# Attention one: a later shift transposition, another order of the first scores, and other waits for the stack loads

## The chip, the cores and the metric

One core of a Trainium2 chip runs the whole program. The time is the device time of one execution in microseconds (us). TensorE (PE) multiplies and transposes, VectorE (DVE), ScalarE (ACT) and GpSimd (POOL) do the rest, SyncE (SP) issues the transfers.

## What is computed

A small language model tower: a token table lookup, attention one, a mixture of experts, attention two, and a feed-forward part with block-quantised values. Only attention one is touched:

```python
h = _L0_tok_ref(x, L0_tok_W)                       # 8 x 1024 tokens, 256 wide
h = h + _L0_attn_ref(_layernorm(h, axis=-1), Wqkv, bqkv, Wr, br)

def _L0_attn_ref(x, Wqkv, bqkv, Wr, br):           # 16 heads of 16
    xh = x.reshape(b, c, h, he).transpose(0, 2, 1, 3)
    qkv = jnp.einsum('bhce,ef->bhcf', xh, Wqkv) + bqkv
    q, k, v = jnp.split(qkv, 3, axis=-1)
    att = jnp.einsum('bhqe,bhke->bhqk', q, k) / jnp.sqrt(jnp.float32(he))
    mask = jnp.tril(jnp.ones((c, c), dtype=att.dtype), k=-1)
    att = jax.nn.softmax(att * mask, axis=-1)      # masked scores are 0, not minus infinity
    out = jnp.einsum('bhqk,bhke->bhqe', att, v)
    return out.transpose(0, 2, 1, 3).reshape(b, c, d) @ Wr + br
```

The masked scores count as zeros in the softmax, so the kernel needs each row's maximum over the scores in front of the diagonal and zero, and a term for the sum of all later values.

## The kernel before

Attention one handles 8 batches in two halves of eight heads each, 16 halves in all, and each half as two groups of four heads (HPG). `window` (L93) writes one pass over a group as a list of events, `plan` (L166) puts the passes together (an even one, gi = 0, then an odd one, gi = 1; the loop runs 14 halves), and each engine's program walks the same list in order. A pass has 32 positions. Position 4·kt + hh holds the score step S(kt, hh): key block kt of 128 keys against all later queries, in two units (128·kt to 512, and 512 to 1024) for kt < 4 and in one for the others, 48 units in all (`score_units`, L56). TensorE writes a unit into one of two `scoresT` banks (L638), ScalarE takes its exponential into `probs` (L495), GpSimd masks the diagonal block (L415), and the value product PV(kt) (L652) follows one key block later. PV(7) runs behind the first step of the next pass.

Between the steps, at positions given by `AT`, the list places the rest:

- MX: the scores of queries against keys for the row maxima, two heads (a pair) at a time, 9 banks for each head, into a ring of four PSUM banks (L688, masks L674), reduced by VectorE (L587). `bank_free` makes the matmul of each use of the ring wait until the use four before it has been read. XT, QK, V, SUF, PT, OT, WR and CT use the same ring in the same order.
- MAX_FINAL: VectorE reduces to m (L577), GpSimd splits m in two bf16 parts c1 and c2 and adds them to cf (L451, L453, L455). CT: TensorE transposes c1, c2 of a pair (L721) after waiting for cf (`cm_ok`), VectorE copies it to `ct` (L591) and SyncE puts it as shift rows into the query stack Qs of the next pass (L359). EQ: ScalarE takes exp(-cf) (L526).
- In an even pass: the layer norm of the next half (VectorE's statistics, GpSimd's rstd, VectorE's xn L564), its transposition XT (L702), the Q/K projection QK (L706) with ScalarE's copies to `f32part` and `parts` (L512, L513), V (L709), the suffix sums SUF (L716, L718). PT (L726) transposes the value products of the pass before, WR (L734, odd passes) is the output projection.
- LOAD: SyncE writes the next pass's stacks Qs and Ks from `parts` in 24 transfers (L337). It waits for `parts` and until TensorE has done the first 8 score units of the running pass. LOAD_MAX: four transfers of 128 KB fill Qm and Km of one pair (L354, L355), after VectorE's m of that pair.

The stacks Qs and Ks have two buffers, one for each pass. Before the first step that uses a pair of heads (S(0,0), S(0,2)) TensorE waits for that pair's stack loads and shift rows. Before it overwrites `parts` for the next half, ScalarE waits at its first QK copy until all loads that read the old `parts` have landed:

```python
if w == 0 and c == 0:
    act.wait_ge(w_in, 16 * WEIGHTS)
    for s in stack_in:
        wait(act, s, 16 * 12 * 2 * (hb + 1))
```

That copy comes behind position 8 of an even pass, and the loads of the odd pass's stacks are issued in the same even pass. SUF lies behind position 9; its second bank is the one that this copy must free.

Of the kernel before, what the change touches and what calls it, by code (L numbers as in the profile page):

```python
# [17 lines left out]
P = 128  # L18
B, S, D = 8, 1024, 256
# [3 lines left out]
TPB = S // P  # L23
HEADS, HE = 16, 16
HALVES = 2 * B
HPG = 4
# [6 lines left out]
PAIRS_MX = HPG // 2  # L33
# [17 lines left out]
MAX_BANKS = len(MAX_PLAN)  # L51
FUTURE = -2.0 ** 126
SCORE_BANKS, RING_BANKS = 2, 4


def score_units(kt, hh):  # L56

    if kt < TPB // 2:
        u = 2 * (HPG * kt + hh)
        return [(u, P * kt, 512), (u + 1, 512, S)]  # L60
    return [(TPB * HPG + HPG * (kt - TPB // 2) + hh, P * kt, S)]


STAGE = 2 * HPG * S
UNITS = TPB * HPG + TPB // 2 * HPG
# [4 lines left out]
def wait_apart(eng, *waits):  # L70


    values = [value if isinstance(value, int) else eng.to_reg(value) for _, value in waits]
    if not all(isinstance(value, int) for value in values):
        eng.wait_ge(waits[0][0], 1)
    for (sem, _), value in zip(waits, values):
        eng.wait_ge(sem, value)
# [4 lines left out]


AT = {
    0: {"LN_STATS": 1, "LN_NORM": 3, "XT": 6, "PV_COPY": 0, "TMP": 0, "PT": 5, "OT": 21, "WR": 22, "RSUM": 5, "SUF": 9, "QK": 8, "QK_STEP": 2, "MID_LAG": 2, "V": 12, "VG": 0, "LOAD": 11, "MX": 6, "MX_END": 29, "MX_CURVE": 1.2},
    1: {"PV_COPY": 0, "TMP": 0, "PT": 2, "WR": 1, "V": 8, "VG": 6, "LOAD": 6, "MX": 3, "MX_END": 28, "MX_CURVE": 1.2},
    "V_IN": 0, "WR_IN": 1,
}
ALONE = {"LN_STATS": 0, "LN_NORM": 1, "XT": 2, "QK": 8, "QK_STEP": 1, "MID_LAG": 1, "V": 12, "PV_COPY": 1, "TMP": 2, "PT": 5, "OT": 11,
# [3 lines left out]
def window(gi, ot, wr, tail, prologue, v, scores, following, load_max=False):  # L93


    others = {}
    pos_of = AT[gi] if scores else ALONE

    def at(pos, *events):
        others.setdefault(min(pos, 31), []).extend(events)  # L100

    if prologue:
        at(pos_of["LN_STATS"], ("LN_STATS",))
        at(pos_of["LN_NORM"], ("LN_NORM",))
        at(pos_of["XT"], ("R", "XT", "act", 0), ("R", "XT", "act", 1))
    if tail:
        at(pos_of["PV_COPY"], ("PV", -1, 7), ("PV_COPY", -1))
        at(pos_of["TMP"], ("TMP", -1))
        at(pos_of["PT"], ("R", "PT", "dve", -1, 0), ("R", "PT", "dve", -1, 1), ("OM", -1))
    if ot:  # L110
        at(pos_of["OT"], ("R", "OT", "act", 0), ("R", "OT", "act", 1))
    if wr:
        for j in range(4):
            at(pos_of["WR"] + (j // 2 if scores else 0), ("R", "WR", "dve", j))
    if gi == 0 and scores:
        at(pos_of["RSUM"], ("RSUM",))
        at(pos_of["SUF"], ("R", "SUF", "dve", 0), ("R", "SUF", "dve", 1))
    if prologue:
        for n in range(4):
            at(pos_of["QK"] + n * pos_of["QK_STEP"], ("R", "QK", "act", n // 2, n % 2))  # L120
            at(pos_of["QK"] + n * pos_of["QK_STEP"] + pos_of["MID_LAG"], ("MID", n // 2, n % 2))
    if v:
        at(pos_of["V"], ("R", "V", "dve", 0), ("R", "V", "dve", 1))
    if following:
        at(pos_of["VG"], ("VG",))
        at(pos_of["LOAD"], ("LOAD",))
        if not scores:
            at(pos_of["LOAD"], *(("LOAD_FIRST", p) for p in range(PAIRS_MX)))
        uses = []
        for p in range(PAIRS_MX):  # L130
            for k in range(MAX_BANKS):
                uses.append([("R", "MX", "dve", 2 * p, k), ("R", "MX", "dve", 2 * p + 1, k)])
                if p and k == 3:
                    uses[-1] += [("R", "CT", "dve", p - 1)]
                if p and k == 4 and load_max:
                    uses[-1] += [("LOAD_MAX", p - 1)]
            uses[-1] += [("MAX_FINAL", p)]
        uses.append([("R", "CT", "dve", PAIRS_MX - 1), ("EQ",)] + ([("LOAD_MAX", PAIRS_MX - 1)] if load_max else []))
        lo, hi = pos_of["MX"], pos_of["MX_END"]
        for n, u in enumerate(uses):  # L140
            at(int(lo + (hi - lo) * (n / len(uses)) ** pos_of["MX_CURVE"]), *u)
    events = []
    for pos in range(32 if scores else max(others, default=-1) + 1):
        if scores:
            kt, h = divmod(pos, HPG)
            events.append(("S", kt, h))
            if h == HPG - 1 and kt >= 1:
                events.append(("PV", 0, kt - 1))
        events += others.pop(pos, [])
    return [(gi,) + e for e in events]  # L150
# [34 lines left out]
def attention_one(nc, dram, h, shared):  # L185
    plans = plan()
    with ExitStack() as ctx:
# [48 lines left out]
        OT = sb("OT", [P, S])  # L236
# [8 lines left out]
        filled, read_dve, read_act = sem("ring_filled"), sem("ring_read_dve"), sem("ring_read_act")  # L245
        mv_ok, rstd_ok, xn_ok = sem("mv_ok"), sem("rstd_ok"), sem("xn_ok")
        rest_ok, mid_ok, parts_ok = sem("rest_ok"), sem("mid_ok"), sem("parts_ok")
# [5 lines left out]
        m_ok, cm_c, cm_ok, eq_ok = sem("m_ok"), sem("cm_c"), sem("cm_ok"), sem("eq_ok")  # L253
# [4 lines left out]
        def wait(eng, s, value):  # L258

            if isinstance(value, int) and value <= 0:  # L260
                return
            eng.wait_ge(s, value)
# [39 lines left out]
        with nc.Block() as block:  # L302

            @block.sync
            def _(sp):
# [16 lines left out]
                def run(section, hb, it):  # L322
                    num = numbers(section, it)
                    for e in plans[section]:
                        g, par = 2 * hb + e[0] + 1, (e[0] + 1) % 2
                        if e[1] == "LOAD":
                            if section == "loop":
                                wait_apart(sp, (parts_ok, 4 * (hb + 1 + e[0])), (st_ok, UNITS * (g - 1) + 2 * HPG))
                            else:
                                sp.wait_ge(parts_ok, 4 * (hb + 1 + e[0]))  # L330
                                wait(sp, st_ok, UNITS * (g - 1) + 2 * HPG)
                            for hh in range(HPG):
                                rows = slice(16 * (HPG * par + hh), 16 * (HPG * par + hh) + 16)

                                def put(stack, lo, n, src):

                                    sp.dma_start(stack[lo:lo + 16 * n, par, hh, :], src).then_inc(stack_in[hh // 2], 16)  # L337

                                put(Qs, 0, 3, parts[rows, 0, 0:3, :])
                                put(Ks, 0, 3, parts[rows, 1, 0:1, :].broadcast_to([16, 3, S]))  # L340
                                put(Qs, 48, 2, parts[rows, 0, 0:2, :])
                                put(Ks, 48, 2, parts[rows, 1, 1:2, :].broadcast_to([16, 2, S]))
                                put(Qs, 80, 1, parts[rows, 0, 0:1, :])
                                put(Ks, 80, 1, parts[rows, 1, 2:3, :])
                        elif e[1] in ("LOAD_FIRST", "LOAD_MAX"):
                            p, first = e[2], e[1] == "LOAD_FIRST"
                            if first:
                                wait_apart(sp, (parts_ok, 4 * (hb + 2)))
                            else:
                                wait_apart(sp, (parts_ok, 4 * (hb + 2)), (m_ok, PAIRS_MX * g + p + 1))  # L350
                            lo = 16 * (HPG * (par if first else 1 - par) + 2 * p)
                            rows = slice(lo, lo + 32)
                            for i in range(2):
                                sp.dma_start(Qm[i:P:2, p, :], parts[rows, 0, i:i + 1, :].broadcast_to([32, 2, S])).then_inc(max_in[p], 16)  # L354
                                sp.dma_start(Km[i:P:2, p, :], parts[rows, 1, 0:2, :]).then_inc(max_in[p], 16)  # L355
                        elif e[1] == "R" and e[2] == "CT":
                            read(sp, section, num, e)
                            for i in range(2):
                                sp.dma_start(Qs[STACK:ROWS, par, 2 * e[4] + i, :],  # L359
                                             ct[16 * i:16 * i + 16, par, e[4], :]).then_inc(shift_in[e[4]], 16)  # L360
# [259 lines left out]
            def _(pe):  # L620
# [4 lines left out]
                def run(section, hb, it):  # L625
                    num = numbers(section, it)
                    for e in plans[section]:
# [13 lines left out]
                        elif kind == "PV":  # L641
# [3 lines left out]
                            if kt == 0:  # L645
                                wait(pe, pvS_ok, 2 * v)
                                pe.wait_ge(vg_ok, v + 1)
                            pe.wait_ge(mask_ok, 32 * v + 4 * kt + 4)
                            pe.wait_ge(exp_ok, UNITS * v + score_units(kt, HPG - 1)[-1][0] + 1)
                            for lo, hi in ((P * kt, 512), (512, S)) if kt < 4 else ((P * kt, S),):  # L650
                                for hh in range(HPG):
# [44 lines left out]
                        elif kind == "R":  # L696
# [20 lines left out]
                                    if t < TPB - 1:  # L717
                                        ins = nc.tensor.matmul(o, ones[:], Rsum[:, t, :], start=False, stop=True)  # L718
                            elif e[2] == "CT":
                                pe.wait_ge(cm_ok, PAIRS_MX * g + e[4] + 1)  # L720
                                ins = nc.tensor.transpose(out[0:32, 0:64].bitcast(BF16),  # L721
                                                          c12[:, nxt, 2 * e[4]:2 * e[4] + 2].rearrange("p h c t -> p (h c t)"), ident_b[:])
                            elif e[2] == "PT":
# [1051 lines left out]
```

## Time and profile before

| | us |
|---|---|
| median of three runs | 3225.5 |
| lowest, highest | 3218.67, 3233.48 |
| profiled execution, its time | 3221.99 |
| profiled execution, its span | 3220.2 |
| TensorE busy | 2746.9 |
| VectorE, ScalarE, GpSimd busy | 2115.3, 1592.7, 1727.9 |

The span is that of the core's instructions; the time has what lies around it. Attention one fills the first half, from its first score at 95.8 us to the last at 1730.4. A row of a timeline gives start and duration in us, the engine, the line of the kernel, what is written and read, the count of merged instructions, and in brackets the idle time before it and what ended it. The granted clock is a share of TensorE's full speed: 1.00 is 2.4 GHz and 0.50 is 1.2 GHz.

### The profile page before, as it was taken

Reading aid. Unit: us, or ns where it says so; the run is one execution under the profiler, and the core shown is the slowest. Engines: PE = TensorE matmul, PEld = TensorE weight load, DVE = VectorE, ACT = ScalarE, POOL = GpSimd, SP = SyncE. Lnnn points to the kernel's source line nnn. Section 1 sums busy time; section 2 is a strip of 40 time slices with the busy share of each in tenths; the row PEclk is TensorE's granted clock in tenths of the full one; section 3 lists DMA queues with packets and bytes.
Section 4 is the critical chain, followed back from the end, with each engine's and each line's share of the span. In section 5 each row is a group of like instructions: output and inputs, shape, how many; then the busy total and the mean of one; then the engine's idle time right before and its main releaser. Section 6 shows DMA issues by size and latency. Waiting matters only on the chain. (4 is left out here: it accounts for less than half of the span.)

```text
span 3220.2 us, 61044 instructions
## 1 busy us (share of the span) xinstructions
PE 2746.9 (85%) x15254; PEld 1578.1 (49%) x15318; DVE 2115.3 (66%) x5668; ACT 1592.7 (49%) x3630; POOL 1727.9 (54%) x3076
## 2 busy tenths in 40 slices
PE   1678888888888888888887699989898979999999
PEld 1223433333333443334334466666666656666666
DVE  2545655665656656656563799989898976565554
ACT  1345555555545555455553265555555545444444
POOL 3663443334333343334433487777777757767766
PEclk7678888888878888888887799999999989999999
DMA  3352324333342323423243000000000000000000
GB/s 52 84 107 44 53 43 59 56 49 46 50 62 47 51 46 52 66 43 52 43 59 128 1 1 1 1 1 1 1 1 1 1 1 10 15 16 15 15 15 19
DMA packets 81303, 113.30 MB, mean 35 GB/s; under 512 B 25100, under 2 KB 37144, under 8 KB 80536
## 3 DMA queue, kind: packets, MB, share of 16 engines
q1 hardware_dynamic: 76360, 101.44, 19.5%
q0 software_dynamic: 3072, 8.39, 0.9%
q10 hardware_dynamic: 1744, 2.16, 0.2%
q14 instruction: 95, 0.78, 0.1%
q8 instruction: 32, 0.52, 0.1%
HBM read 18.98 MB, written 8.39 MB: 8 GB/s over the span
## 5 line engine op out<-in xcount | busy, mean ns | idle before, releaser
L495 ACT ACTIVATE probs<-scoresT 128x512 f32<-128x512 f32 (+3 forms) x1536 | 693.1, 490 | 610.2 <-PE scoresT L638 580.5
L587 DVE TENSOR_REDUCE cand<-ring 128x4 f32<-128x512 f32 x1152 | 720.4, 683 | 261.2 <-PE ring L688 197.6
L415 POOL TENSOR_SCALAR_AFFINE_SELECT probs<-probs 128x128 f32<-128x128 f32 x1024 | 294.3, 293 | 619.3 <-ACT probs L495 608.9
L638 PE MATMUL scoresT<-stage 98*128 98x512 bf16 (+3 forms) x1536 | 506.7, 386 | 70.4 <-ACT probs L495 61.8
L652 PE MATMUL pv<-probs,Vg 128*32 128x512 f32 (+3 forms) x3072 | 352.9, 569 | 5.0 <-POOL probs L415 5.0
L688 PE MATMUL ring<-Km,Qm 64*128 64x512 bf16 (+2 forms) x1792 | 251.4, 320 | 80.8 <-DVE cand L587 41.5
L638 PEld LDWEIGHTS scoresT<-stage 98*128 98x128 bf16 x1536 | 131.2, 100 | 375.3 <-ACT probs L495 241.4
L1115 PE MATMUL mm<-w_W,hT 128*128 128x256 f32 x1024 | 258.5, 398 | 9.1 <-ACT z L1203 3.5
L1135 PE MATMUL mm<-w_W,x2T 128*128 128x512 f32 x512 | 242.2, 596 | 0.3 <-DVE x L1354 0.2
L688 PEld LDWEIGHTS ring<-Km,Qm 64*128 64x128 bf16 x1792 | 83.8, 95 | 323.7 <-DVE cand L587 145.1
L1196 ACT ACTIVATE hT<-mmT,w_be,w_g 128x128 f32<-128x128 f32 x512 | 185.9, 469 | 90.2 <-PE mmT L1126 90.2
L1115 PEld LDWEIGHTS mm<-w_W,hT 128*128 128x128 f32 x1024 | 207.1, 202 | 36.2 <-issue 0.3
L1557 PE MATMUL down_ps<-q_down,turned 128*128 128x256 f32 (+1 forms) x768 | 201.5, 396 | 2.3 <-ACT turned L1587 2.3
L1611 POOL TENSOR_TENSOR val<-val,power 128x960 f32<-128x960 f32 (+2 forms) x68 | 129.1, 1899 | 112.7 <-ACT power L1598 112.6
L1519 PE MATMUL gate<-q_w_gate,turned 128*128 128x352 f32 x512 | 174.0, 462 | 0.7 <-ACT turned L1582 0.5
L1519 PE MATMUL up<-q_w_up,turned 128*128 128x352 f32 x512 | 172.8, 460 | 0.0
L1557 PEld LDWEIGHTS down_ps<-q_down,turned 128*128 128x128 f32 (+1 forms) x768 | 134.9, 189 | 68.2 <-issue 43.4
L1570 ACT ACTIVATE act_g<-gate 128x352 f32<-128x352 f32 x128 | 59.4, 464 | 209.0 <-PE gate L1519 202.6
L1263 POOL TENSOR_TENSOR u<-z,w_g 128x512 f32<-128x512 f32 x128 | 160.2, 1273 | 2.1 <-ACT z L1203 2.1
L1203 ACT ACTIVATE z<-mm,nmw,rw 128x256 f32<-128x256 f32 x256 | 124.2, 573 | 48.5 <-POOL nmw L1280 48.2
L1135 PEld LDWEIGHTS mm<-w_W,x2T 128*128 128x128 f32 x512 | 98.2, 192 | 87.5 <-issue 83.3
L652 PEld LDWEIGHTS pv<-probs,Vg 128*32 128x32 f32 x3072 | 78.4, 119 | 124.2 <-issue 98.0
(254 smaller groups left out, 5367.5 us busy)
## 6 DMA issues: line engine op xcount, KB each, us to landing
stage<-parts SPq DMA_DIRECT2D x256, 96.0 KB
stage<-parts SPq DMA_DIRECT2D x256, 64.0 KB
Qm<-parts SPq DMA_DIRECT2D x128, 128.0 KB
Km<-parts SPq DMA_DIRECT2D x128, 128.0 KB
stage<-parts SPq DMA_DIRECT2D x256, 32.0 KB
out<-result SPq DMA_DIRECT2D x64, 128.0 KB, 1.7
stage<-ct SPq DMA_DIRECT2D x128, 4.0 KB
w_W<-in_W SPq DMA_DIRECT2D x4, 512.0 KB
```

The costliest lines, as they stand in the source:

```text
L415: nc.gpsimd.affine_select(out=d, in_=d, compare_op=ALU.is_gt, fill=0.0, base=0, pattern=[[1, P]], channel_multiplier=-1).then_inc(mask_ok, 1)
L495: nc.scalar.activation(probs[:, n % 8, lo:hi], scoresT[u % SCORE_BANKS][:, lo % 512:(hi - 1) % 512 + 1], ACT.Exp, scale=SOFT).then_inc(exp ...
L587: ins = nc.vector.tensor_reduce(c, src[:].rearrange("p (t a b) -> p t a b", t=c.shape[1], b=P), AX.X, ALU.max)
L638: nc.tensor.matmul(scoresT[u % SCORE_BANKS][:, lo % 512:(hi - 1) % 512 + 1], Ks[0:ROWS, gi, hh, P * kt:P * kt + P], Qs[0:ROWS, gi, hh, lo: ...
L652: ins = nc.tensor.matmul(pv[32 * hh:32 * hh + 32, lo:hi], Vg[:, par, kt, hh, :], probs[:, (4 * kt + hh) % 8, lo:hi], start=(kt == 0), stop ...
L688: ins = nc.tensor.matmul(out[x][:, P * at:P * (at + n)], Qm[half[x], hh // 2, P * i:P * i + P], Km[half[x], hh // 2, P * j:P * (j + n)], s ...
L1115: ins = nc.tensor.matmul(o, hT[:, 2 * e + c, :], w["W2"][:, c, e, :], start=False, stop=(e % 2 == 1 and c == 1))
L1135: ins = nc.tensor.matmul(mm1[p][:], x2T[same][:, c, :], w["W1"][:, c, 2 * p:2 * p + 2, :].rearrange("p e n -> p (e n)"), start=False, stop ...
L1196: nc.scalar.activation(hT[:, j, :], mmT[p][:, P * k:P * k + P], ACT.Relu, bias=w["be1"][:, j:j + 1], scale=w["g1"][:, j:j + 1]).then_inc(h ...
L1263: nc.gpsimd.tensor_tensor(u[same][:, 2 * p:2 * p + 2, :], z[same][:, 2 * p:2 * p + 2, :], w["g2"][:].rearrange("p (e n) -> p e n", e=E4)[: ...
L1519: ins = nc.tensor.matmul(out[:, 0:HALF], turned[par][:, 5 + c, :], wt[:, c, HALF * a:HALF * a + HALF], start=(c == 0), stop=(c == 1))
L1557: ins = nc.tensor.matmul(down[:, 0:D], turned[1 - u][0:rows, at, :], w["down"][0:rows, k, :], start=(n == 0), stop=(n == CHUNKS - 1))
```

## The change

The order of the first scores becomes S(0,0), S(0,1), S(1,0), S(1,1), S(0,2), S(0,3), S(1,2), S(1,3); `score_units` and the wait for the masks follow it. MX begins at position 4 instead of 6 in even passes and at 2 instead of 3 in odd ones. The first pair's CT comes one MX bank later. The last pair's CT and EQ go behind position 31, so behind all scores. CT waits for c2 (`cm_c`) instead of cf. LOAD waits for 16 score units instead of 8. LOAD_MAX follows its pair's MAX_FINAL and waits for the pair's last MX matmul (`filled`) instead of m. By the new plan the events of an even pass from position 4 on are: S(0,2) MX MX (two pairs of banks); S(0,3) PT; S(1,2) XT MX; S(1,3) PV(0) MX; S(2,0) QK MX; S(2,1) SUF MX. Before they were: S(1,0); S(1,1) PT; S(1,2) XT MX MX; S(1,3) PV(0) MX; S(2,0) QK MX; S(2,1) SUF MX.

```diff
+ORDER = [(kt, hh) for kt in range(TPB) for hh in range(HPG)]
+ORDER[2:6] = [(1, 0), (1, 1), (0, 2), (0, 3)]
 def score_units(kt, hh):
+    n = ORDER.index((kt, hh))
     if kt < TPB // 2:
-        u = 2 * (HPG * kt + hh)
-        return [(u, P * kt, 512), (u + 1, 512, S)]
-    return [(TPB * HPG + HPG * (kt - TPB // 2) + hh, P * kt, S)]
+        return [(2 * n, P * kt, 512), (2 * n + 1, 512, S)]
+    return [(TPB // 2 * HPG + n, P * kt, S)]
+def masks_before(kt):
+    return 1 + max(ORDER.index((kt, hh)) for hh in range(HPG))
...
-    0: {... "MX": 6, "MX_END": 29, "MX_CURVE": 1.2},
-    1: {... "MX": 3, "MX_END": 28, "MX_CURVE": 1.2},
+    0: {... "MX": 4, "MX_END": 28, "MX_CURVE": 1.1},
+    1: {... "MX": 2, "MX_END": 28, "MX_CURVE": 1.1},
...
-                if p and k == 3:
+                if p and k == 4:
                     uses[-1] += [("R", "CT", "dve", p - 1)]
-                if p and k == 4 and load_max:
-                    uses[-1] += [("LOAD_MAX", p - 1)]
-            uses[-1] += [("MAX_FINAL", p)]
-        uses.append([("R", "CT", "dve", PAIRS_MX - 1), ("EQ",)] + ([("LOAD_MAX", PAIRS_MX - 1)] if load_max else []))
+            uses[-1] += [("MAX_FINAL", p)] + ([("LOAD_MAX", p)] if load_max else [])
...
+        at(31, ("R", "CT", "dve", PAIRS_MX - 1), ("EQ",))
...
-            kt, h = divmod(pos, HPG)
+            kt, h = ORDER[pos]
...
-                                wait_apart(sp, (parts_ok, 4 * (hb + 1 + e[0])), (st_ok, UNITS * (g - 1) + 2 * HPG))
+                                wait_apart(sp, (parts_ok, 4 * (hb + 1 + e[0])), (st_ok, UNITS * (g - 1) + 4 * HPG))
...
-                                wait_apart(sp, (parts_ok, 4 * (hb + 2)), (m_ok, PAIRS_MX * g + p + 1))
+                                last = [x for x in plans[section] if x[0] == e[0] and x[1:3] == ("R", "MX")
+                                        and x[4:6] == (2 * p + 1, MAX_BANKS - 1)][0]
+                                wait_apart(sp, (parts_ok, 4 * (hb + 2)), (filled, num(last[-1][0], 0) + 1))
...
-                            pe.wait_ge(mask_ok, 32 * v + 4 * kt + 4)
+                            pe.wait_ge(mask_ok, 32 * v + masks_before(kt))
...
-                                pe.wait_ge(cm_ok, PAIRS_MX * g + e[4] + 1)
+                                pe.wait_ge(cm_c, 2 * (PAIRS_MX * g + e[4]) + 2)
```

## Rows read from the trace of the kernel before

**Rows 1.** The page: busy time and share of TensorE, and its granted clock in 40 slices.

```profile
PE 2746.9 (85%) x15254; PEld 1578.1 (49%) x15318; DVE 2115.3 (66%) x5668; ACT 1592.7 (49%) x3630; POOL 1727.9 (54%) x3076
...
PEclk7678888888878888888887799999999989999999
```

**Rows 2.** Stretches, an even and an odd pass: length, busy time by engine, clock, DMA.

```profile
731.22:789.32 58.10, 47.84 (x324) 22.89 (x320) 34.17 (x73) 31.47 (x67) 26.55 (x58) 0.82 0.31 44
789.32:833.62 44.30, 38.96 (x270) 15.45 (x267) 27.51 (x49) 22.93 (x51) 12.69 (x41) 0.85 0.43 62
```

**Rows 3.** Waits over attention one: waiter, what for, total us, times, longest.

```profile
PE ring L721 <- POOL cf L455: 72.3, 32, 4.7
PE ring L716 <- ACT parts L513: 67.7, 15, 4.6
...
ACT f32part L512 <- DMA stage<-parts: 83.0, 14, 6.0
```

**Rows 4.** Timeline, the ends of two passes: TensorE, and SyncE's issues of shift rows.

```profile
727.18 0.29 PE L721 MATMUL ring<-ident_b,c 128*32 128x128 bf16 x1 [2.54 <-POOL cf L455]
...
727.72 1.51 PE L652 MATMUL pv<-probs,Vg 128*32 128x384 f32 x8
...
784.48 0.85 PE L652 MATMUL pv<-probs,Vg 128*32 128x384 f32 x8
787.16 0.23 PE L721 MATMUL ring<-ident_b,c 128*32 128x128 bf16 x1 [1.83 <-POOL cf L455]
...
727.74 1.39 SPq L359 DMA_DIRECT2D stage<-ct  x2
```

**Rows 5.** Timeline of an even pass: SyncE's stack loads, ScalarE's first projection copy, TensorE's suffix sums.

```profile
737.11 15.31 SPq L337 DMA_DIRECT2D stage<-parts  x24
...
754.62 0.69 ACT L512 ACTIVATE f32part<-ring,b_q 128x512 f32<-128x512 f32 x1 [5.96 <-DMA stage<-parts]
...
755.93 0.80 PE L716 MATMUL ring<-Vh,upper 128*128 128x128 f32 x2 [4.57 <-ACT parts L513]
```

**Rows 6.** Timeline of TensorE in the same even pass, from its fifth step on.

```profile
737.22 1.58 PE L638 MATMUL scoresT<-stage 98*128 98x384 bf16 x3 [0.20 <-ACT probs L495]
...
739.41 1.91 PE L726 MATMUL ring<-ident,pvS 128*128 128x128 f32 x8
741.12 0.95 PE L638 MATMUL scoresT<-stage 98*128 98x384 bf16 x2
741.86 1.82 PE L702 MATMUL ring<-ident,xn 128*128 128x128 f32 x8
...
744.81 0.55 PE L638 MATMUL scoresT<-stage 98*128 98x384 bf16 x2
```

**Rows 7.** Timeline of VectorE in the same stretch.

```profile
740.09 2.15 DVE L564 TENSOR_SCALAR xn<-h,mv,rstd 128x128 f32 x8 [2.45 <-POOL rstd L423]
742.15 0.44 DVE L608 TENSOR_TENSOR acc<-ring,tmp 128x272 f32<-128x272 f32 x1
...
744.14 2.48 DVE L587 TENSOR_REDUCE cand<-ring 128x4 f32<-128x512 f32 x4 [0.59 <-PE ring L688]
```

**Rows 8.** Timeline of TensorE at the start of the odd pass.

```profile
791.71 3.36 PE L734 MATMUL ring<-w_r,OT 128*128 x8
...
795.34 1.04 PE L726 MATMUL ring<-ident,pvS 128*128 128x128 f32 x8
796.21 1.89 PE L734 MATMUL ring<-w_r,OT 128*128 x8
```

**Rows 9.** Stretches of a few us, columns as in rows 2: the clock is the last but two.

```profile
727.00:731.00 4.00, 3.56 (x22) 0.95 (x22) 0.21 (x1) 1.50 (x6) 1.90 (x8) 0.50 0.10 16
...
739.00:742.00 3.00, 2.99 (x12) 2.44 (x13) 1.91 (x8) 1.25 (x3) 1.33 (x3) 0.50 0.88 96
...
746.00:751.00 5.00, 5.00 (x37) 2.70 (x30) 3.20 (x6) 1.03 (x3) 2.24 (x7) 1.00 0.88 108
...
756.00:760.00 4.00, 4.00 (x18) 3.28 (x19) 0.67 (x2) 0.64 (x2) 1.37 (x2) 0.50 0.00 0
```

More of the change, by code:

```diff
@@ L84 @@
 AT = {
-    0: {"LN_STATS": 1, "LN_NORM": 3, "XT": 6, "PV_COPY": 0, "TMP": 0, "PT": 5, "OT": 21, "WR": 22, "RSUM": 5, "SUF": 9, "QK": 8, "QK_STEP": 2, "MID_LAG": 2, "V": 12, "VG": 0, "LOAD": 11, "MX": 6, "MX_END": 29, "MX_CURVE": 1.2},
-    1: {"PV_COPY": 0, "TMP": 0, "PT": 2, "WR": 1, "V": 8, "VG": 6, "LOAD": 6, "MX": 3, "MX_END": 28, "MX_CURVE": 1.2},
+    0: {"LN_STATS": 1, "LN_NORM": 3, "XT": 6, "PV_COPY": 0, "TMP": 0, "PT": 5, "OT": 21, "WR": 22, "RSUM": 5, "SUF": 9, "QK": 8, "QK_STEP": 2, "MID_LAG": 2, "V": 12, "VG": 0, "LOAD": 11, "MX": 4, "MX_END": 28, "MX_CURVE": 1.1},
+    1: {"PV_COPY": 0, "TMP": 0, "PT": 2, "WR": 1, "V": 8, "VG": 6, "LOAD": 6, "MX": 2, "MX_END": 28, "MX_CURVE": 1.1},
     "V_IN": 0, "WR_IN": 1,
@@ L327, in run @@
                             if section == "loop":
-                                wait_apart(sp, (parts_ok, 4 * (hb + 1 + e[0])), (st_ok, UNITS * (g - 1) + 2 * HPG))
+                                wait_apart(sp, (parts_ok, 4 * (hb + 1 + e[0])), (st_ok, UNITS * (g - 1) + 4 * HPG))
                             else:
                                 sp.wait_ge(parts_ok, 4 * (hb + 1 + e[0]))
-                                wait(sp, st_ok, UNITS * (g - 1) + 2 * HPG)
+                                wait(sp, st_ok, UNITS * (g - 1) + 4 * HPG)
                             for hh in range(HPG):
```

## The prediction

> I call the work on one group of four heads a **pass**. A half is an even and an odd pass, and each pass issues 32 score steps S(kt,h), numbered 0 to 31. Times inside a pass count from its first score matmul.
>
> **What bounds the kernel now.** I read the page first [rows 1]: TensorE is busy 85% of the span, no other engine is near that, and its granted clock is lowest in the first half of the slices, which is attention one. Then I measured one half of the loop by the table of stretches [rows 2]: 58.10 us for the even pass, 44.30 for the odd one, 102.40 together, and the 14 halves of the loop repeat it, so one half stands for them. The reader should see there that TensorE's matmuls are busy 47.8 + 39.0 = 86.8 of the 102.4 us, at a granted clock of 0.82 and 0.85.
>
> The sums of waits over attention one [rows 3] then name two stops of TensorE of like size. Both are short in one pass and regular: 32 waits of the shift's transposition (L721) for GpSimd's cf, 72.3 us; and 15 waits, 67.7 us, of the suffix matmuls (L716) for ScalarE's copies of the Q/K projection. The second is really a transfer: ScalarE itself waits 83.0 us, 14 times some 6 us, at L512 for the stack loads. The change attacks the first stop and moves the start of the load behind the second. That is the whole case.
>
> [Rows 4] show the first stop at the ends of an even and of an odd pass: 1.83 and 2.54 us idle before the transposition, 4.37 a half. [Rows 5] show the second as a chain: SyncE issues the 24 loads of the stacks from 737.11 on, 5.89 us into the pass; that takes 15.31 us; 2.20 us after the last issue ends (752.42) ScalarE goes on with L512 (754.62, after 5.96 us idle); 1.31 us later TensorE resumes (755.93, after 4.57 us idle). So TensorE resumes 18.82 us after the first load is issued, and in 14 of 15 even passes nothing else decides it.
>
> **The change, step by step.**
>
> *The last pair's transposition* goes from step 26 or 27 to behind step 31 and no longer waits for cf, only for c2. cf came 2.5 us after TensorE had run out of released work; in the new place there are four or five score steps and one or two value products before it, so I count the wait as gone: 15 × 4.37 = 65.6 us in the 15 halves with a projection, and of the 72.3 in all about 4 more from the first and last passes. Cover: the shift rows are now needed by S(0,2), the fifth step of the next pass. Behind the transposition lie DVE's copy, two issues of 1.39 us together [rows 4] and, by the stack loads' 2.20 us, a landing: some 4 us. The four steps ahead of it take 6.0 us at ScalarE's pace (the fifth begins at 737.22) [rows 6], so it stays hidden. If the new LOAD_MAX (four issues, by the loads' 15.31/24 = 0.64 us each) were still on the queue ahead, it would be late by about 0.6 us.
>
> *Scores in the new order* are the same 48 matmuls. The small eq exponential and the transposition now lie at the boundary; ScalarE sets the pace of the first steps, so I add 0.2 a pass, 0.4 a half.
>
> *LOAD_MAX* starts earlier and is off every path in [rows 5]; it is ahead of the shift on SyncE's queue, costed above. Nothing.
>
> *LOAD waits for 16 score units instead of 8.* In an even pass the old eight were steps 0 to 3, over at 5.8 us. The new sixteen are steps 0 to 7, so S(1,3) must be done, and SyncE's queue holds nothing else that could be earlier. In the kernel before, S(1,3) ends at 745.36 [rows 6], 14.14 us into the pass; that alone would move the load by 8.25 us. The new plan puts more ahead of S(1,3): four key-score banks (MX of heads 0 and 1) go before PT, and the ring has four banks. So PT must wait until DVE has reduced them, and DVE is held until it has written xn, at 742.24, 11.02 into the pass [rows 7]. From there: one reduction is 2.48/4 = 0.62 us, so PT starts at 11.7. At the lower clock: PT 1.91 (13.6), S(1,2) 0.74 (741.12 to 741.86; 14.35), XT 1.82 (16.2), one MX pair 0.57 (two of them lie between XT's end, 743.68, and 744.81; 16.75), S(1,3) 0.55 to 0.95, I take 0.65 [rows 6]. LOAD starts at 17.4, **11.5 us later**. At the full clock the eight PT transposes take 1.04 [rows 8]; then DVE is the chain: four reductions to 13.5, PT's two adds of 0.44 [rows 7] with a reciprocal between them to about 14.65, an MX pair and S(1,3) about 0.95, LOAD at 15.6, 9.7 us later. I take 11.5: the row it is nearest to is PT in an even pass, 1.91, and TensorE idles some 2 us right before PT in the new plan.
>
> The chain behind (18.82 us) is SyncE's issue time and stays. So TensorE resumes 11.5 us later. By then it has done five MX pairs instead of four: one pair fewer afterwards, worth between nothing and its two reductions, 1.24; I take 0.8, a little above TensorE's 0.57. In an odd pass the same delay costs nothing: its loads run from about 14.4 to 30 us and are wanted at 44.
>
> *The clock.* The granted clock is 1.00 in the middle of a pass and 0.50 from just behind the stop of [rows 4] until 742 at least [rows 9]: TensorE stands idle 2.5 us, and what follows runs at 1.2 GHz, not 2.4. Without that stop the value products at the pass ends could stay fast: the 128x384 product takes 1.51 slow (727.72) and 0.85 fast (784.48) [rows 4], 0.66 less; for the smaller 128x256 one behind it I estimate 0.45 by the same ratio. That is 1.1 in an odd pass's end and up to 0.5 in an even one's, whose 128x384 product is fast already. In the odd pass the output projection (8 matmuls) takes 3.36 slow and 1.89 fast [rows 8]: 1.5 more if the clock holds through the boundary, which is even odds, as ScalarE paces the scores there; so 0.7 to 0.8. Together 2.4 of at most 3.4 a half, and at least 0.
>
> The Trainium skill ("TensorE: Matmul & The Clock Gate", Part 1) says that the throttled state is the default and that activity releases it. By that rule the removed stop could give back a second sum. But it speaks against the change too, since the new stop in front of the suffix matmuls is longer. The trace already has 0.50 behind the present stop of 4.57 us from 756 to 760 [rows 9], so lengthening it adds no second slow stretch; with or without the page the sum stands.
>
> **Sum for a half:** +11.5 − 0.8 − 4.4 − 2.4 + 0.4 = +4.3 us. Fifteen halves: +64; the first and last passes' extra waits −4; together +60. The profiled execution took 3222.0 (span 3220.2), so 3282. The median of the three runs, 3225.5, is 3.5 above it, within their spread of 15; I leave 3282.
>
> **Rivals.**
> 1. *The clock holds everywhere*, in the even pass's start too. For: its slow stretch begins right behind the removed stop. Against: ScalarE paces the scores there, and TensorE waits 0.20 for it ahead of a step even when it is slow [rows 6]. Then the delay is 9.7 and the whole 3.4 comes back, plus 0.6 in the boundary products: 9.7 − 0.8 − 4.4 − 4.0 + 0.4 = +0.9; 15 times that, less 4, is +10: 3232, no change; up to 3240 if a part of it is missing.
> 2. *No clock comes back*, because the ends of the passes are paced by ScalarE and the clock falls anyway, and the MX pair done earlier saves nothing: 11.5 − 4.4 + 0.4 = +7.5; 15 times that, less 4, is +108: 3330.
> 3. *The delay is small and the kernel gets faster.* Mechanism: S(1,3) keeps its place of before, 8.25 us, because PT isn't held by the ring's banks, and with the clock of rival 1 PT and XT ahead of it are 0.87 [rows 6, 8] and by the same ratio some 0.8 shorter, so the delay is 6.6: 6.6 − 0.8 − 4.4 − 4.0 + 0.4 = −2.2 a half, 3185. It decides from a delay below 8.8 us with the clock whole (below 7.2 with 2.4). Against: four banks, two MX pairs and DVE's place in its own program.
> 4. *The wait isn't removed but moved*: S(0,2) waits for the shift's landing behind LOAD_MAX, say 1 us in each of 30 passes: 3312.
>
> **How the numbers follow.** Forecast 0.62, rival 1 0.13, rival 2 0.13, rival 3 0.06, rival 4 0.06. What a measurement can tell from no change is about 0.5%, 16 us: above 3242 is slower, below 3209 faster. Slower: 0.62 + 0.13 + 0.06 and a third of rival 1, 0.85. Same: 0.09. Faster: 0.06. The range leaves out rival 3 and the upper part of rival 2, and takes in most of rival 1: 3236 to 3325.
>
> **What would show it.** In the changed profile: LOAD's first issue in an even pass at 17 us instead of 5.9; L512's wait for the transfer at about 14 us or more instead of 6; the suffix matmuls' stop at 12 us instead of 4.6, 15 times, about 170 us in all; hardly any idle before L721's transposition; a half of 105 to 109 us. If LOAD starts before 14 us, the ring argument is wrong. If the slow clock ends before 742 or its like, rival 1 holds. If S(0,2) shows waits for "stage<-ct", it is rival 4. If a projection's copy waits no longer than before, the whole forecast falls.

## The result: 1.65% slower

The changed kernel took 3280.56 us (median, 3277.69 to 3282.02), the kernel before in the same comparison 3227.89. The ratio is 1.0165, 95% interval 1.0139 to 1.0191. Forecast were 3282 and a range of 3236 to 3325. By the two medians the change costs 53 us; the forecast was 60.

The page of the changed kernel: TensorE's busy time is 70 us less than in [rows 1], the span 60 us more. So the time isn't in TensorE's work. Its clock row differs from that before by at most one tenth in any slice.

```profile
span 3280.2 us, 61044 instructions
...
PE 2676.9 (82%) x15254; PEld 1546.9 (47%) x15318; DVE 2100.8 (64%) x5668; ACT 1590.0 (48%) x3630; POOL 1728.9 (53%) x3076
...
PEclk7678888888888888888888699999999999999999
```

The table of stretches for one even and one odd pass of the changed kernel (columns as in [rows 2]). The even pass is 8.6 us longer than in [rows 2], the odd one 5.2 shorter; a half takes 105.86 instead of 102.40. In the odd pass TensorE's busy time falls from 38.96 to 34.95 and the granted clock rises from 0.85 to 0.97: the same matmuls, faster.

```profile
758.20:824.93 66.73, 46.76 (x320) 22.46 (x320) 33.03 (x73) 31.32 (x67) 26.66 (x59) 0.79 0.27 40
824.93:864.06 39.13, 34.95 (x271) 13.87 (x266) 27.56 (x50) 22.81 (x51) 12.61 (x41) 0.97 0.47 67
```

TensorE's and ScalarE's waits over attention one, changed kernel. Line numbers are 10 higher than before (L726 is the suffix sum, L736 PT). The stop for the transposition [rows 3] has gone from the list. The stop behind the loads has grown from 67.7 to 192.3 us, ScalarE's own from 83.0 to 199.5, and two waits are new or nearly so: the value product for the masks (38.5 us; 5.0 before) and PT for VectorE's reductions (27.9).

```profile
PE ring L726 <- ACT parts L523: 192.3, 15, 12.9
PE scoresT L648 <- ACT probs L505: 82.7, 194, 4.1
PE pv L662 <- POOL probs L425: 38.5, 32, 3.6
PE ring L736 <- DVE cand L597: 27.9, 14, 2.5
...
ACT f32part L522 <- DMA stage<-parts: 199.5, 14, 14.3
```

The chain of [rows 5] in the changed kernel, in the even pass that begins at 758.2: SyncE's loads, ScalarE's copy, TensorE's suffix sums. What to see is that the loads start 15.8 us into the pass instead of 5.9 and take as long as before (15.35 against 15.31), and that TensorE again resumes 18.87 us after the first of them.

```profile
774.04 15.35 SPq L345 DMA_DIRECT2D stage<-parts  x24
...
791.59 0.69 ACT L522 ACTIVATE f32part<-ring,b_q 128x512 f32<-128x512 f32 x1 [14.33 <-DMA stage<-parts]
...
792.91 0.80 PE L726 MATMUL ring<-Vh,upper 128*128 128x128 f32 x2 [12.95 <-ACT parts L523]
```

### The profile page after: what moved, and what is told of

The parts are those of the page before. It is cut to its first block and busy times, and to the rows that moved or that the text cites. A ratio compares the mean times of both kernels' runs of the same rounds, so it can differ in the third digit from the quotient of the medians.

```text
span 3280.2 us, 61044 instructions
## 1 busy us (share of the span) xinstructions
PE 2676.9 (82%) x15254; PEld 1546.9 (47%) x15318; DVE 2100.8 (64%) x5668; ACT 1590.0 (48%) x3630; POOL 1728.9 (53%) x3076
## 5 line engine op out<-in xcount | busy, mean ns | idle before, releaser
L648 PE MATMUL scoresT<-stage 98*128 98x512 bf16 (+3 forms) x1536 | 495.0, 373 | 96.4 <-ACT probs L505 83.5
L662 PE MATMUL pv<-probs,Vg 128*32 128x512 f32 (+3 forms) x3072 | 321.7, 524 | 38.8 <-POOL probs L425 38.8
L726 PE MATMUL ring<-Vh,upper 128*128 128x128 f32 x256 | 66.8, 353 | 192.3 <-ACT parts L523 192.3
L437 POOL TENSOR_TENSOR f32part<-f32part,parts 128x512 f32<-128x512 f32 x64 | 74.0, 1157 | 238.8 <-ACT parts L523 238.8
L611 DVE COPY suf<-ring 128x512 f32<-128x512 f32 x32 | 22.1, 692 | 248.1 <-PE ring L726 233.2
```

The costliest lines, as they stand in the source:

```text
L648: nc.tensor.matmul(scoresT[u % SCORE_BANKS][:, lo % 512:(hi - 1) % 512 + 1], Ks[0:ROWS, gi, hh, P * kt:P * kt + P], Qs[0:ROWS, gi, hh, lo: ...
L662: ins = nc.tensor.matmul(pv[32 * hh:32 * hh + 32, lo:hi], Vg[:, par, kt, hh, :], probs[:, (4 * kt + hh) % 8, lo:hi], start=(kt == 0), stop ...
```

## The experiments

Theory A: the later start of the stack loads costs a us for each us in every even pass, and moving the transposition gives back less than that. Theory B: the new order, the place of the maxima and the new waits cost the time. The lengths of passes below are taken between first score matmuls in the middle of the loop; where they alternate, both are given. Each ratio is to the kernel before as it was timed in the same comparison; that median moves between 3215 and 3228 us, so ratios are compared here, not times.

| kernel | first load, us into an even pass | even + odd pass = half, us | ratio, 95% interval |
|---|---|---|---|
| before | 5.9 | 58.1 + 44.3 = 102.4 | 1 |
| changed | 15.8 | 66.7 + 39.1 = 105.8 | 1.0165 (1.0139 to 1.0191) |
| 1: changed, loads at 12 units | 9.0 | 59.8 + 39.2 = 99.0 | 0.9864 (0.9830 to 0.9898) |
| 2: before, loads at 16 units | 14.3 | 66.2 + 43.1 = 109.2 | 1.0332 (1.0292 to 1.0372) |
| 3: changed, old order, loads at 8 | 5.5 | 55.7 + 39.7 = 95.4 | 0.9702 (0.9669 to 0.9736) |
| 4: changed, transposition back | 16.6 | 67.8 + 41.5 = 109.2 | 1.0360 (1.0325 to 1.0396) |
| 5: as 3, final maximum later | 5.3 to 5.5 | 53.3 or 54.7 + 38.0 | 0.9542 (0.9516 to 0.9568) |
| 6: changed, maxima from position 6 | 13.5 to 13.8 | 63.3 to 64.9 + 38.8 to 40.2 | 1.0083 (1.0057 to 1.0109) |
| 7: as 3, projections later | 5.5 | 52.7 + 39.4 = 92.1 | 0.9546 (0.9520 to 0.9572) |
| 8: changed, wide waits back | 15.8 | 66.7 + 39.1 = 105.8 | 1.0192 (1.0164 to 1.0220) |
| 9: before, transposition alone | 5.5 | 56.5 + 39.1 = 95.6 | 0.9693 (0.9677 to 0.9709) |
| 10: 3, 5 and 7 together | 5.5 | 51.2 or 53.9 + 38.0 | 0.9473 (0.9457 to 0.9489) |
| 11: as 10, maxima from position 6 | 5.1 to 5.5 | 49.3 to 49.8 + 38.0, near 87.5 | 0.9342 (0.9326 to 0.9357) |

**Experiment 1: the loads four units earlier.**

```diff
-(st_ok, UNITS * (g - 1) + 4 * HPG)
+(st_ok, UNITS * (g - 1) + 3 * HPG)
```

> The changed kernel, but the stack loads wait for 12 score units instead of 16 (S(0,2) and S(0,3), the last steps that wait for the stacks, are done with 12). Theory A (the later start of the loads sets the time): unit 12 ends 8.9 us into an even pass instead of 15.7, so the loads start and the suffix sums go on 6.8 us earlier; 15 halves, 102 us less than the changed kernel: about 3178, ratio to the kernel before 0.985. Theory B (the ring order, PT behind four MX banks, and the new waits for masks cost the time): these stay, the ratio stays above 1.01.

Measured: 0.9864, 3168.55 us. The loads start 6.8 us earlier in the even pass, and the half is 6.8 us shorter. SyncE's timeline in an even pass of this kernel (it begins at 704.0), and TensorE's longest wait in it:

```profile
712.98 15.27 SPq L345 DMA_DIRECT2D stage<-parts  x24
```

```profile
PE ring L726 <- ACT parts L523: 6.0, 1, 6.0
```

All else in the pass is as in the changed kernel (PT's stop, the mask wait). One number of the change turns 1.65% slower into 1.4% faster: Theory A. The wait for 16 units was more than the new order needs: S(0,2) and S(0,3), the last steps that wait for the stacks, are done with 12.

**Experiment 2: the kernel before with that wait alone.**

```diff
-(st_ok, UNITS * (g - 1) + 2 * HPG)
+(st_ok, UNITS * (g - 1) + 4 * HPG)
```

> The kernel before, with nothing changed but that the stack loads wait for 16 score units instead of 8. Theory A: the loads start 14.2 us into an even pass instead of 5.9, 8.3 us a half, 15 halves: +124 us, about 3350, ratio 1.038. Theory B: nothing of the ring or of the order is changed, so less than 1%.

Measured: 1.0332, 3318.96 us. The loads start 8.4 us later and TensorE's stop in front of the suffix sums is as long as in the changed kernel (SyncE's timeline in an even pass that begins at 759.3, and TensorE's waits in it):

```profile
773.59 15.27 SPq L337 DMA_DIRECT2D stage<-parts  x24
```

```profile
PE ring L716 <- ACT parts L513: 12.9, 1, 12.9
PE scoresT L638 <- ACT probs L495: 2.1, 7, 0.8
PE ring L721 <- POOL cf L455: 1.8, 1, 1.8
```

The suffix sums resume 8.4 us later, but the half is only 6.8 longer: 1.2 comes back in the odd pass and 0.3 behind the stop. Theory A holds, with four fifths of the price. Why the odd pass is shorter was not examined.

**Experiment 3: is the new order needed?**

```diff
-ORDER[2:6] = [(1, 0), (1, 1), (0, 2), (0, 3)]
...
-(st_ok, UNITS * (g - 1) + 4 * HPG)
+(st_ok, UNITS * (g - 1) + 2 * HPG)
```

> The changed kernel with the scores in their old order, S(0,0) to S(0,3) first, and the stack loads at 8 units as before; the transposition stays behind all scores. Theory A: loads start at 5.5 us instead of 15.8, 10.3 less a half; S(0,2) comes 3.1 us into a pass, the shift rows land at about 3.7, so some 0.8 a pass comes on top: -8.7 a half, about 3150, ratio 0.976. Rival (the order is needed, as the shift's way through VectorE, SyncE and the transfer is longer): 3 us or more a pass of waiting for the shift, ratio 0.99 or above.

Measured: 0.9702, 3115.27 us; expected was 0.976. S(0,2), which needs the shift rows, is the third step here. The timeline of TensorE at a pass start shows what it waits for: the exponentials, not the rows.

```profile
683.13 0.22 PE L730 MATMUL ring<-ident_b,c 128*32 128x128 bf16 x1
683.59 0.60 PE L647 MATMUL scoresT<-stage 98*128 98x512 bf16 x2 [0.24 <-issue]
684.12 0.43 PE L661 MATMUL pv<-probs,Vg 128*32 128x128 f32 x8
684.67 1.09 PE L647 MATMUL scoresT<-stage 98*128 98x512 bf16 x2
686.62 1.10 PE L647 MATMUL scoresT<-stage 98*128 98x512 bf16 x2 [0.86 <-ACT probs L504]
```

So the rows are there by 686.62, 3.5 us after the transposition's start, behind two score steps and the copies of the value products. I had put the landing 0.6 us later. The new order covers a wait that isn't there, and its price is the later loads. The half is 10.4 us shorter than the changed kernel's, and the loads start 10.3 earlier. Experiment 1's kernel, with the new order, is in line: its loads start 3.5 us later than here and its half is 3.6 longer. So the order itself gains nothing that can be seen here.

**Experiment 4: the transposition back in the list.**

```diff
+        uses.append([("R", "CT", "dve", PAIRS_MX - 1), ("EQ",)])
...
-        at(31, ("R", "CT", "dve", PAIRS_MX - 1), ("EQ",))
...
-                                pe.wait_ge(cm_c, 2 * (PAIRS_MX * g + e[4]) + 2)
+                                pe.wait_ge(cm_ok, PAIRS_MX * g + e[4] + 1)
```

> The changed kernel with the last transposition and the exponential of cf back behind the last MX bank (one bank later in the list, position 27), waiting for cf again. Theory A with my sum: the stop of 1.8 and 2.5 us comes back and with it the slow clock at the pass ends, 6.8 a half, +100 us: about 3380, ratio 1.047. Rival (the stop only hid other waits that come in its place): +30 us or less, ratio below 1.026.

Measured: 1.0360, 3327.1 us. The stop comes back (89.3 us over attention one) and the mask wait shrinks from 38.5 to 3.7: the half is 3.4 longer, half of what I had expected. From this alone I concluded that the transposition was worth 3.4; experiment 9 put that right.

```profile
PE ring L731 <- POOL cf L465: 89.3, 32, 7.7
...
PE pv L662 <- POOL probs L425: 3.7, 3, 2.2
```

**Experiment 5: the new mask wait.**

```diff
-            uses[-1] += [("MAX_FINAL", p)] + ([("LOAD_MAX", p)] if load_max else [])
+            uses[-1] += ([("MAX_FINAL", p)] if p < PAIRS_MX - 1 else []) + ([("LOAD_MAX", p)] if load_max else [])
...
+        at(28 if scores else 31, ("MAX_FINAL", PAIRS_MX - 1))
         at(31, ("R", "CT", "dve", PAIRS_MX - 1), ("EQ",))
```

> The third experiment's kernel (old score order, loads at 8 units) with the last pair's final maximum (VectorE's m, GpSimd's c1, c2, cf) placed behind S(7,0) instead of behind the last bank of maxima; nothing in the pass waits for it any more but the transposition at its end. Theory (GpSimd stands waiting for m in front of the masks, so PV(6) waits 1.1 us at the end of each pass): 2.3 us a half go, 15 halves: 35 us, ratio to the kernel before 0.959 against 0.970. Rival (the masks are late for another reason, or the exponentials take over as the wait): ratio 0.966 or more.

Measured: 0.9542 against 0.9702. The mask wait falls from 45.4 us over attention one to 3.8, the odd pass is 1.7 us shorter, the even one 1.0 or 2.4. The cause is visible in GpSimd's timeline of the changed kernel: it stands 2.20 us waiting for m, in front of five masks that it then does without a pause; TensorE's value product waits for them.

```profile
756.24 0.20 POOL L461 CAST c<-m 128x16 bf16<-128x16 f32 x1 [2.20 <-DVE m L587]
...
756.99 1.30 POOL L425 TENSOR_SCALAR_AFFINE_SELECT probs<-probs 128x128 f32<-128x128 f32 x5
...
757.34 0.64 PE L662 MATMUL pv<-probs,Vg 128*32 128x256 f32 x8 [1.15 <-POOL probs L425]
```

**Experiment 6: the maxima no longer ahead of PT.**

```diff
-"MX": 4, "MX_END": 28
+"MX": 6, "MX_END": 28
```

> The changed kernel with the maxima's banks from position 6 of an even pass on, as before, instead of 4. Theory of my sum (four banks of maxima in front of PT hold it until VectorE has reduced them, and with it S(1,3) and the loads): TensorE's 2.0 us stop in front of PT is gone and the loads start at about 13.9 us instead of 15.8; with a pair fewer done ahead, 1 us a half less, ratio 1.012 or lower. Rival (what is ahead of S(1,3) is paced by VectorE's layer norm anyway): the loads start at 15.5 us or later.

Measured: 1.0083, 3249.84 us. The loads start at 13.5 us instead of 15.8, the stop before PT is gone, and the half is 1.1 to 2.9 us shorter. The ring argument holds: four banks of maxima ahead of PT held back S(1,3), and with it the loads, by 2.3 us.

**Experiment 7: the projections two positions later.**

```diff
-"QK": 8, "QK_STEP": 2
+"QK": 10, "QK_STEP": 2
```

> The third experiment's kernel (old score order, loads at 8 units) with the Q/K projections two positions later (10, 12, 14, 16). Theory (ScalarE's first projection copy waits for the loads' landing, 3.45 us in that kernel, and TensorE 2.1 us behind it): two more score steps and a value product lie ahead of the copy, so the wait is gone, 2 us a half: ratio 0.961 against 0.970. Rival (the projection's own chain, GpSimd's and ScalarE's four parts, then ends too late for the rest of the pass): no gain.

Measured: 0.9546 against 0.9702, 3.3 us a half and not 2. ScalarE's wait for the loads is no longer among its longest, and the suffix sums don't stand behind the projection's copy any more. What is left is a stop of 1.9 us in each even pass, in front of a bank of maxima, which waits for the same copy.

**Experiment 8: the two narrowed waits.**

```diff
-(filled, num(last[-1][0], 0) + 1)
+(m_ok, PAIRS_MX * g + p + 1)
...
-pe.wait_ge(cm_c, 2 * (PAIRS_MX * g + e[4]) + 2)
+pe.wait_ge(cm_ok, PAIRS_MX * g + e[4] + 1)
```

> The changed kernel with the two narrowed waits widened again: the transposition waits for cf instead of c2, the loads of Qm and Km for m instead of the last matmul of the maxima. Theory: neither is on a path in the new places; the ratio to the kernel before stays that of the changed kernel, 1.0165, within 0.3%. Rival (the reload ahead of the shift on SyncE's queue now holds the shift): S(0,2) waits for the shift rows, 1 us or more a pass, ratio 1.025.

Measured: 1.0192, interval 1.0164 to 1.0220, which overlaps with that of the changed kernel; the half is the same 105.8. Neither wait is on a path in the loop. The first half of attention one differs: 126.7 us in this kernel's trace, 132.5 in the changed kernel's. Why was not examined.

**Experiment 9: the transposition alone, on the kernel before.**

```diff
-        uses.append([("R", "CT", "dve", PAIRS_MX - 1), ("EQ",)] + ([("LOAD_MAX", PAIRS_MX - 1)] if load_max else []))
+        uses.append([("LOAD_MAX", PAIRS_MX - 1)] if load_max else [])
...
+        at(31, ("R", "CT", "dve", PAIRS_MX - 1), ("EQ",))
```

> The kernel before with one part of the change alone: the last transposition and the exponential of cf behind step 31; it still waits for cf; order, maxima, loads and all other waits stay. By the sum of the prediction (4.4 us of stop, 2.4 of clock, less 0.4): 6.4 a half and 4 more, -100 us, ratio 0.969. By the difference that the fourth experiment showed (3.4 a half, since the mask wait takes part of the stop's place): -55 us, ratio 0.983. If the score order were needed for it: S(0,2) waits for the shift rows, ratio 0.99 or more.

Measured: 0.9693, 3128.36 us: 6.8 us a half; by the prediction's terms it was 6.4. This one move is 3% and the good part of the change: the kernel of experiment 3, which has the earlier maxima and the narrowed waits besides, takes 95.4 us a half against 95.6. Stretches of this kernel, even and odd pass: the odd pass has the clock of the changed kernel's (0.97) and nearly its busy time, 34.64 against 34.95. TensorE's busy time in a half is 81.18 us, 5.6 less than before.

```profile
698.70:755.25 56.55, 46.54 (x321) 22.44 (x322) 33.05 (x73) 31.18 (x67) 26.70 (x59) 0.84 0.31 46
755.25:794.30 39.05, 34.64 (x268) 14.21 (x268) 27.72 (x50) 22.83 (x51) 12.61 (x41) 0.97 0.48 70
```

**Experiment 10: experiments 3, 5 and 7 in one.** No new edit.

> Old score order, loads at 8 units, the last final maximum behind S(7,0) and the projections from position 10, all on the changed kernel. If both waits (masks, loads) are separate: 0.970 less 0.016 less 0.016, ratio 0.938 to 0.942. If one of them was cover for the other (the pass ends earlier, so the loads are late again): 0.95.

Measured: 0.9473. The gains don't add up in full (0.9542 and 0.9546 against 0.9702 would give 0.939). PT's stop for VectorE's reductions stays (31.5 us) and now is the largest stop but one.

**Experiment 11: the tenth kernel with the maxima from position 6.**

```diff
-"QK": 10, ... "MX": 4, "MX_END": 28
+"QK": 10, ... "MX": 6, "MX_END": 28
```

> The tenth kernel with the maxima from position 6 of an even pass. Theory (TensorE's 2.4 us stop in front of PT is the ring's): it goes, some 1.5 to 2 us a half after the later maxima are paid, ratio 0.93. Rival (VectorE, which reduces all maxima, becomes the pace of the rest of the pass): no gain or a loss.

Measured: 0.9342, 3014.02 us, the fastest of all, 213 us below the kernel before in the same comparison. A half takes about 87.5 us, 3.5 less than the mean of the tenth kernel's, where 1.5 to 2 were expected. Its even and odd pass, and TensorE's waits in the even one: nothing over 2.8 us is left, and the clock is 0.93 and 1.00.

```profile
647.10:696.60 49.50, 43.93 (x321) 20.45 (x321) 33.05 (x73) 31.34 (x67) 26.06 (x58) 0.93 0.36 52
696.60:734.65 38.05, 34.50 (x267) 13.77 (x268) 27.62 (x50) 23.06 (x52) 13.11 (x43) 1.00 0.50 72
```

```profile
PE scoresT L648 <- ACT probs L505: 2.8, 7, 1.1
PE ring L698 <- ACT parts L523: 0.9, 1, 0.9
```

## Why the prediction came out right, step by step

**The direction and the place were right.** The loads' start sets when TensorE resumes, 18.8 us after it in both kernels, and experiments 1 and 2 show it from both sides. Theory B fell with experiment 1 as the explanation, though two things in it have a price of their own: the mask wait (experiment 5) and the maxima ahead of PT (experiment 6). No rival occurred: the clock is 0.50 at the start of the even pass of the changed kernel too (rival 1), a half's matmuls are busy 81.7 us instead of 86.8, so clock did come back (rival 2), S(1,3) comes later than before (rival 3), and in the loop no score step waits for the shift rows (rival 4). The lower bound of 3236 was said to take in most of rival 1; it leaves out its own figure, 3232.

**The delay was sized 11.5 and is 9.9.** Two links of my replay were too slow. PT started 10.8 us into the pass (769.07), not at 11.7, because VectorE was done with xn at 10.1 instead of 11.0. I had taken its chain from [rows 7] as fixed. But its start in the kernel before holds a collision: the copy of Vg took 1.36 us beside GpSimd's multiplication tmp, and 0.43 in the changed kernel, where GpSimd begins that multiplication 0.55 us after the copy has begun. The copy also starts 1.1 us into the pass instead of 1.7, so VectorE's statistics are done 1.6 us earlier; 0.9 of that is left at xn, since a mask stands in front of rstd on GpSimd. No experiment took the collision out alone. Rows of the kernel before, then of the changed one:

```profile
732.91 1.36 DVE L572 COPY Vg<-Vh 128x512 f32<-128x512 f32 x1 [5.20 <-PE pv L652]
...
732.86 1.13 POOL L464 TENSOR_TENSOR tmp<-suf,eq 128x544 f32<-128x544 f32 x1
```

```profile
759.33 0.43 DVE L582 COPY Vg<-Vh 128x512 f32<-128x512 f32 x1 [1.03 <-PE pv L662]
...
759.88 1.13 POOL L474 TENSOR_TENSOR tmp<-suf,eq 128x544 f32<-128x544 f32 x1
```

And from PT's start to the first load it took 5.0 us and not 5.7: S(1,2) follows PT's start by 1.76 instead of 1.91, XT takes 1.50 (771.58 to 773.08) instead of 1.82, the MX pair 0.32 (773.08 to 773.40) instead of 0.57. TensorE's wait before PT is 1.95 us, against some 2 in the prediction. TensorE's timeline in the changed kernel:

```profile
769.07 1.97 PE L736 MATMUL ring<-ident,pvS 128*128 128x128 f32 x8 [1.95 <-DVE cand L597]
770.83 0.95 PE L648 MATMUL scoresT<-stage 98*128 98x384 bf16 x2
771.58 1.57 PE L712 MATMUL ring<-ident,xn 128*128 128x128 f32 x8
773.08 0.39 PE L698 MATMUL ring<-Km,Qm 64*128 64x512 bf16 x2
773.40 0.55 PE L648 MATMUL scoresT<-stage 98*128 98x384 bf16 x2
```

**The transposition and the clock were sized −6.8 together, −6.4 with the boundary's 0.4, and by experiment 9 are −6.8.** The sum is about right, its parts are not. I had missed a wait: with the transposition gone, the value product PV(6) waits 1.1 us in each pass for masks that stand behind GpSimd's wait for m (experiment 5). The saving has to pay for that too, 1.1 and 0.9 us in the two passes of experiment 9, so what is not the stop itself gave by estimate some 2 us more than my 2.4 (6.8 + 2.1 − 4.4 = 4.5). The busy time fits: it falls by 5.6 us a half in experiment 9 and by 5.1 in the changed kernel. The odd pass, for which my terms come to some 4.2 less, is 5.2 shorter, and its stretch from 828 to 860 is at 1.00 throughout (below). A part of the saving may be the collision above, which I had not foreseen: in the middle of the loop the copy of Vg takes 1.36 us in every even pass of the kernels whose transposition stands in the list (before, experiments 2 and 4), and 0.43 in every even pass of the ten others. In the changed kernel, undone again, the same move is worth only 3.4 (experiment 4). That the price depends on the rest of the pass is shown; why it is half there was not examined.

**The slow stretch behind the stop was right.** The stretches show the clock at 0.50 behind the longer stop, over 792.9 to 796.3, as it was over 756 to 760 before [rows 9], and at 1.00 again later. The clock falls while TensorE stands (0.59 over 781 to 792), which costs nothing then, and the removed short stops gave back more than their own length (6.8 us for 4.4). The Trainium skill ("TensorE: Matmul & The Clock Gate", Part 1) says that the throttled state is the default and that activity releases it; these rows agree. Why the clock is at 0.50 from 759 to 772.5, with no long stop ahead of it, is not shown.

```profile
759.00:764.00 5.00, 3.90 (x15) 0.73 (x7) 3.69 (x17) 4.48 (x10) 2.67 (x6) 0.50 0.01 2
...
781.00:792.00 11.00, 0.00 (x0) 0.00 (x0) 0.00 (x0) 0.41 (x1) 0.00 (x0) 0.59 0.78 90
792.90:796.30 3.40, 3.39 (x16) 3.17 (x18) 0.00 (x0) 0.72 (x2) 1.41 (x2) 0.50 0.00 0
...
828.00:860.00 32.00, 29.49 (x230) 11.74 (x228) 25.30 (x45) 18.96 (x41) 9.39 (x31) 1.00 0.51 66
```

**The agreement to 2 us is luck.** In a half the delay came out 1.6 us below its term, and all other terms together gave 6.5 (9.9 less 3.4) instead of 7.2. What comes behind the stop in an even pass is 1.3 us shorter; less the removed stop of 1.83 and with the new mask wait of 1.1, some 0.7 are left for the earlier MX pair (sized 0.8) and the clock. So a half in the loop grew by 3.4 us, not 4.3: 15 halves give 51, not 64. For the first and last passes I had put −4, and they gave +9: the first half grew by 9.3 us (123.2 to 132.5), 5.9 more than those in the loop, and the last, which has no projection, by 2.6 (79.7 to 82.3, to the end of its last score), where I had expected a gain. Two misses of 13 us cancel. The forecast was also added to one execution of 3222.0 us; from the median of the kernel before, 3227.89, the same 60 us would give 3288. Why the first and last halves grew wasn't examined; experiment 8's first half of 126.7 shows that this growth isn't a constant of the new order.

## What to carry to other kernels

A step that is put later for one engine's sake takes its conditions along: here two score steps were moved for a transfer that was there 3.5 us after its start, and the semaphore wait that was raised to cover them, by twice as many units as they needed, moved a load chain of 18.8 us, which was already late. Before reordering to cover a wait, measure whether the wait exists; and look for who else counts the events that are being renumbered. A short stop of TensorE can cost more than its length: stops of 4.4 us a half gave back 6.8 here, though new waits of some 2 us came in their place.

## What the runs showed of the hardware

- VectorE's 128x512 copy within the on-chip memory took 1.36 us when GpSimd's multiplication (732.86 to 733.99) had begun 0.05 us before it, and 0.43 us where the multiplication began only after the copy's end (759.33 to 759.76, then 759.88). The slow copy ended 0.28 us behind GpSimd's instruction. It was so in every even pass in the middle of the loop. The Trainium skill ("SBUF — State Buffer", section "SBUF: two separate sides") says that the two engines share one pair of ports, held by whoever starts first for the whole instruction. The order of the starts and the copy's end behind GpSimd's agree with it; whether GpSimd would wait for a copy that had started first is shown in neither trace.
- Nine of the thirteen kernels here settle, in the middle of the loop, on halves of 92.1, 95.4, 95.6, 99.0, 102.4, 105.8 (two kernels) and 109.2 us (two kernels), steps of about 3.4 us. A delay of 8.4 us cost 6.8 (experiment 2), and the same transposition was worth 6.8 in one place and 3.4 in another (experiments 9 and 4), so an edit's us isn't always a us. The others (experiments 5, 6, 10 and 11) vary from half to half. What makes the loop settle was not tried.
